# Sharing six PSUM banks between two attention passes: four and two in place of three and three

## The reference

```python
# part a, for each of 3 scales; 16 heads of width 8
q, k, v = proj(Wq, bq), proj(Wk, bk), proj(Wv, bv)
scores = einsum('bhqd,bhkd->bhqk', q, k) * sqrt(8)
scores = where(causal, -inf, scores)
m = max(scores, axis=-1)
e = exp(scores - m)
out = (e / (sum(e) + 1e-6)) @ v           # then @ Wo.T + bo, layer norm
# the 3 scales are joined by Wout and a second layer norm
# part b: one such attention, scores / sqrt(8) plus slope[h] * (key - query)
# layers: 6 x (windowed attention, window 32, heads of width 64; then a gated feed-forward)
```

## Time and profile before

| | |
|---|---|
| time, median of 3 | 5068.25 us |
| the profiled execution's own time | 5069.97 us |
| its span, first to last instruction | 5068.2 us |
| PE busy | 4611.6 us, 91% |
| DVE busy | 3758.7 us, 74% |
| ACT busy | 3280.8 us, 65% |
| POOL busy | 2201.0 us, 43% |
| mean granted clock of PE | 0.941 |

### The profile page before, as it was taken

How to read it: one execution, slowest core, us unless ns; L and a number is a source line. 1 busy time by engine, 2 the same in 40 slices (tenths; PEclk the granted TensorE clock), 3 DMA queues, 4 the chain that set the end, 5 groups by cost and what they waited for, 6 DMA issues and landing times. The chain is left out here.

```text
span 5068.2 us, 123490 instructions
## 1 busy us (share of the span) xinstructions
PE 4611.6 (91%) x50168; PEld 2728.4 (54%) x50168; DVE 3758.7 (74%) x5802; ACT 3280.8 (65%) x5283; POOL 2201.0 (43%) x1271
## 2 busy tenths in 40 slices
PE   5999989869999999999999499789999999999997
PEld 2333334336666666666666234256666666666664
DVE  4877777258888888888887287278888887888884
ACT  1666666437777777777776146367777777777774
POOL 1111000046656565565654010166556565656551
PEclk5999999779999999999999679699999999999998
DMA  3221120000000000000000220000000000000000
GB/s 79 42 41 34 31 36 3 2 32 10 10 15 10 5 21 2 19 7 15 10 6 2 48 41 2 32 10 10 2 15 10 15 10 15 10 2 24 2 6 9
DMA packets 70041, 87.85 MB, mean 17 GB/s; under 512 B 22533, under 2 KB 44289, under 8 KB 68865
## 3 DMA queue, kind: packets, MB, share of 16 engines
q1 hardware_dynamic: 67720, 76.41, 6.5%
q10 hardware_dynamic: 1728, 3.15, 0.3%
HBM read 65.11 MB, written 13.63 MB: 16 GB/s over the span
## 5 line engine op out<-in xcount | busy, mean ns | idle before, releaser
L1077 PE MATMUL ps<-l_wqk,l_xa 128*128 128x512 f32 x1536 | 768.3, 623 | 51.7 <-DVE l_rs L1523 40.2
L674 DVE TENSOR_REDUCE a_pm<-ps 128x1 f32<-128x512 f32 (+3 forms) x912 | 561.7, 657 | 204.2 <-PE ps L568 199.1
L1184 PE MATMUL ps<-l_yb,l_mh 128*128 128x256 f32 x3072 | 709.8, 381 | 0.0
L772 ACT ACTIVATE a_pt<-ps 128x512 f32<-128x512 f32 x864 | 475.2, 600 | 328.0 <-PE ps L574 325.9
L1480 POOL TENSOR_TENSOR l_pn<-l_pe,l_rl 128x1024 f32<-128x1024 f32 x192 | 365.2, 1902 | 616.0 <-DVE l_rl L1561 616.0
L1184 PEld LDWEIGHTS ps<-l_yb,l_mh 128*128 128x128 f32 x3072 | 564.3, 190 | 71.5 <-issue 2.4
L1324 ACT ACTIVATE l_sq<-ps 128x1024 f32<-128x1024 f32 x384 | 389.9, 1015 | 317.4 <-PE ps L1077 317.4
L1523 DVE TENSOR_TENSOR l_rs<-ps,l_tab 128x512 f32<-128x512 f32 x768 | 491.0, 681 | 0.0
L1077 PEld LDWEIGHTS ps<-l_wqk,l_xa 128*128 128x128 f32 x1536 | 277.0, 194 | 384.5 <-issue 337.1
L1471 POOL TENSOR_TENSOR l_qkn<-l_rc,l_rn 128x1024 f32<-128x1024 f32 x192 | 386.4, 2013 | 203.3 <-DVE l_rn L1541 203.3
L1463 POOL TENSOR_TENSOR l_rc<-l_rc,l_rs 128x1024 f32<-128x1024 f32 x192 | 451.5, 2352 | 41.5 <-DVE l_rs L1523 41.5
(11 more groups left out here) (222 smaller groups left out, 8771.5 us busy)
## 6 DMA issues: line engine op xcount, KB each, us to landing
l_wqk<-in_lWqkv SPq DMA_DIRECT2D x24, 512.0 KB, 3.6
scratch<-a_parts SPq DMA_DIRECT2D x12, 768.0 KB, 4.2
a_qs<-scratch SPq DMA_DIRECT2D x72, 128.0 KB
a_ks<-scratch SPq DMA_DIRECT2D x60, 128.0 KB
l_wvt<-in_lWvT SPq DMA_DIRECT2D x12, 512.0 KB, 5.0
l_wo<-in_lWo SPq DMA_DIRECT2D x12, 512.0 KB, 7.2
l_w<-in_lW SPq DMA_DIRECT2D x12, 341.0 KB, 2.9
scratch<-b_parts SPq DMA_DIRECT2D x4, 768.0 KB, 4.9
```

The costliest lines, as they stand in the source:

```text
L674: nc.vector.tensor_reduce(to, src, AX.X, ALU.max).then_inc(s1_free, 1)
L772: nc.scalar.activation(pt[:, K % 3, n - GROUPS[k][0], :], ps[:, 3 + N2 % 3, :], ACT.Exp).then_inc(s2_free, 1)
L1077: last = nc.tensor.matmul(ps[:, x, :], xa[:, u, o:o + P], wqk[:, a * INNER + x * CH:a * INNER + (x + 1) * CH], start=True, stop=True)
L1184: last = nc.tensor.matmul(ps[:, 6, 0:2 * P], mh[:, h, :], yb[:, n % 2, h, :], start=h == 0, stop=h == LH - 1, skip_group_check=True)
```

## The change

The first pass gets banks 0 to 3 and the second pass banks 4 and 5. PE issues an item of the first pass when the item four before it has been read, and one of the second pass when the item two before it has been read. Matmuls, reductions, exponentials, their order and all other waits stay as they are.

```diff
-                                bank1 = N1 % 3
+                                bank1 = N1 % 4
...
-                                if N1 >= 3:
-                                    pe.wait_ge(s1_free, N1 - 2)
+                                if N1 >= 4:
+                                    pe.wait_ge(s1_free, N1 - 3)
...
-                                bank2 = 3 + N2 % 3
+                                bank2 = 4 + N2 % 2
...
-                                if N2 >= 3:
-                                    pe.wait_ge(s2_free, N2 - 2)
+                                if N2 >= 2:
+                                    pe.wait_ge(s2_free, N2 - 1)
...
-                            src = ps[:, N1 % 3, 0:len(item) * w].rearrange("p (j n) -> p j n", n=w)
+                            src = ps[:, N1 % 4, 0:len(item) * w].rearrange("p (j n) -> p j n", n=w)
...
-                            nc.scalar.activation(pt[:, K % 3, n - GROUPS[k][0], :], ps[:, 3 + N2 % 3, :], ACT.Exp).then_inc(s2_free, 1)
+                            nc.scalar.activation(pt[:, K % 3, n - GROUPS[k][0], :], ps[:, 4 + N2 % 2, :], ACT.Exp).then_inc(s2_free, 1)
```

## The result

The changed kernel takes 5156.49 us, the median of four runs (5148.00 to 5165.98), against 5071.82 for the kernel before in four runs: 1.0164 times as long, with a 95% interval of 1.0151 to 1.0177. The forecast was 5136 with a range of 5095 to 5200. Direction, mechanism and range were right; the loss was 85 us where 68 were forecast. Between the two profiled executions it is 89 us (5159.29 against 5069.97), and 86 of them lie in the 28 mixed steps, where the sum had 58. The four steps with a second pass alone are 3 us longer, the first-pass-only steps 3 us shorter, and the layers together 6 us longer (0.2%).

A forecast was written before the change was run, and what follows sets the result against it. No engine is full; in-order PE, 91% busy, sets the pace when it waits. Mixed steps lose 43 us in "a" and 15 in "b", second-pass-only steps 10: 68 us, so 5138, or 5136 against the median; range 5095 to 5200.

The forecast's parts named there:

- second pass alone: Four steps without a first pass: two banks cost 0.5 us a group, five groups, 2.5 us a step, 10 us.
- C at 1.13 us after A: Second-pass matmul of a group's third item waits for the first item's exponential: 0.48 + 0.60 + 0.05, formerly 0.44 us.
- D at 1.62: Second-pass matmul of a group's fourth item starts 0.49 us after the third's, 1.62 us after the first's, formerly 1.22.
- The group 0.40 longer: Group of four items, 22-25, in a mixed step: grows by 1.62 - 1.22 = 0.40 us, passed on in full.
- plain: Mixed steps without side work, like q = 1: seven groups lose 2.8 us a step; 8 in "a", 4 in "b".
- q = 0: Mixed steps where projections cover items 10 to 19: loss 1.4 us each, four counted in "a".
- q = 2: Mixed steps where a 0.66 us side piece hides the wait in most groups: loss 1.4 us each, five in "a".
- q = 3: Mixed steps with, in "a", a layer norm that stops everything anyhow: 1.6 us each, five; "b", without norm, 2.4.
- The cover by side pieces: Side work between a group's items hides the new wait, so q = 0 and q = 2 steps lose 1.4 us, not 2.8.
- the first rival: PE's clock falls too: 66 us more in plain mixed steps, about 5205; 5170 for half, 5290 in all 28; chance 0.16.
- ACT has enough slack: Rival: ACT, idle 272 of 769 us in mixed steps of "a", can give a bank away; 5068, no change; chance 0.06.
- DVE's waits decide: Rival: second pass does not hold PE, and its waits for DVE's maxima go; 5070 - 35 = 5035; chance 0.04.

The follow-up runs named there:

- e1: Against the kernel before: second pass cut from three banks to two, first pass kept at three, bank 3 idle; 5156.53 us (1.0148).
- e3: The kernel before, three and three banks, with each second-pass exponential taking only the first 256 of its 512 columns; 5007.66 us (0.9870).
- e4: The changed kernel, four and two banks, with each second-pass exponential taking only the first 256 of its 512 columns; 5064.64 us (0.9978).

## Why the prediction was right, and where it was off

**The second pass with two banks: right, by its own steps.** C at 1.13 us after A: measured 1.23. D at 1.62: measured 1.72. The group 0.40 longer: measured 0.49. The term that was mis-sized is PE's reaction behind a freed bank, read as 0.05 us from a single row; here it is 0.14. e1 shows that this bank is the whole loss, and e3 and e4 that C and D follow ACT's exponential.

**Steps, against the sum.** From the ends of the steps in both traces:

| kind of step | number | forecast | measured |
|---|---|---|---|
| "a", plain | 8 | 22.4 | 27.7 |
| "a", q = 0 | 4 | 5.6 | 8.3 |
| "a", q = 2 | 5 | 7.0 | 8.0 |
| "a", q = 3 | 5 | 8.0 | 18.2 |
| "b", plain | 4 | 11.2 | 18.9 |
| "b", q = 2 and 3 | 2 | 3.8 | 4.3 |
| second pass alone | 4 | 10 | 3.1 |
| first pass alone | 2 | 0 | about -3 |

A plain step whose clock stays at 1.00 lost 2.6 to 3.0 us, with 2.8 forecast, six of them in all: the 0.09 us too little in each group and the groups that hide more than I counted cancel. The cover by side pieces was real, 1.6 us with q = 2 and, with q = 0, 1.9 in two of four (0.9 and 3.6 in the others), against 1.4 and 1.4. With a second pass alone the group was right and its step was not. A long group went from 3.75 to 4.24 us (in the kernel after, below, 1017.22 to 1021.46), the 0.5 of the forecast, but in four groups of a step and not in five; that would be 8 us. And the clock fell later there, with 81 us at the lower level in place of 91, which by an estimate at 0.35 us each hid some 4 of them. So this row came out at 3 and not at 10, a miss that the total hides. One step counted as plain (q = 1, 41.3 us before) holds a second layer norm and lost 1.9.

```profile
1017.22 1.09 ACT L772 ACTIVATE a_pt<-ps 128x512 f32<-128x512 f32 x2 [1.86 <-PE ps L574]
...
1021.46 1.09 ACT L772 ACTIVATE a_pt<-ps 128x512 f32<-128x512 f32 x2 [1.86 <-PE ps L574]
```

**The clock: the step that failed.** The sum had nothing for it, and the first rival too much. The excess sits in the plain steps with a fall of the clock (+5.1 and +6.9 in "a", three of +5.4 in "b") and in the norm steps. The same step of "b" in the kernel after and in e1_3_2, where the clock stayed up:

```profile
3065.00:3099.30 34.30, 29.75 (x306) 11.83 (x305) 23.86 (x41) 21.07 (x38) 1.74 (x5) 0.90 0.01 2
...
3080.00:3085.00 5.00, 4.59 (x47) 1.77 (x40) 2.53 (x4) 2.31 (x5) 0.00 (x0) 0.52 0.01 3
```

```profile
3072.70:3104.70 32.00, 27.16 (x306) 11.15 (x305) 23.82 (x41) 21.10 (x38) 1.74 (x5) 1.00 0.01 2
```

A clock of 0.90 over 34.3 us is 6.9 us at the lower level (1.2 GHz, a granted 0.50), and the step is 2.3 us longer: 0.34 us lost for each of them, since PE's waits fill a part of the slow time. By the same reckoning, step by step, the 28 mixed steps have 53 us at the lower level before and 115 after; 62 more, at 0.34, are 21 of the 28 us by which the sum fell short in them. In the norm steps of "a" it is 31 before and 58 after, which makes 9 us, nearly the whole excess of that row. This is a reckoning over the steps and not an experiment. Its price does not rest on one pair: three more steps that differ between the kernel after and e1_3_2 in the clock alone give 0.33 to 0.37, and two give 0.5. The clock fell more than I gave it, in a minority of the steps and not in the whole stage: my mark for the rival, a granted clock under 0.95, was reached by 0.01. Why it falls in one plain step and stays up in its like is open.

The page "TensorE: Matmul & The Clock Gate" of the Trainium skill, section "A second HAM failure mode: psum-queue depth-cycling", has the rule that PE's short idle stretches between groups can make the clock swing; the trace agrees in that it now swings in more steps than before, and not in that it does so in each step of the pattern: those at 536.4 and 570.0 us hold 1.00.

**The first pass with four banks.** In the norm step L550's wait went and nothing came of it, as forecast. In the first-pass-only steps I counted nothing; they went from 28.2 to 26.5 us (with three banks, in e1, they stay at 28.2), so DVE was in part what they waited for, at a clock of 0.50 too. There are two such whole steps, 3 us in all. The wait of L550 went with three banks as well (e1), so it was the second pass that took it over, and not the fourth bank that removed it.

**The signs.** I wrote that L574 and L563 would be seen waiting for ACT and that the waits of the earlier trace rows would nearly go. Only L550's did. The label was no evidence on either side.

**The rivals.** That ACT has enough slack falls: ACT was idle for a third of the mixed steps, and two banks still cost 85 us. That DVE's waits decide falls for this split: C and D are held by ACT, and taking the fourth bank away again cost nothing. What a fourth bank would gain while the second pass keeps three stays open, since no run has four and three.

## What to carry to other kernels

A bank is held for the distance from one burst's matmul to the end of its reader's work on it, so two of three banks can be too few for an engine that is busy 65% of the time; before moving one, take from the timeline when the reader ends, not how busy it is. A wait behind two engines that end together is booked on one of them: change one side's depth or length before believing the list. And where PE waits for a copy, look at the copy's place in its engine's queue first; here moving two copies by one or two places was worth 1.2 or 1.45%, and none of the three other splits of the banks was worth anything. Then split such a gain by stage and look at the clock of each: about half of this one was clock that came back in 4 steps of 32.

## What the runs showed of the hardware that was not expected

- Value matmuls (128 rows, 32 columns a head, 512 wide, f32) of four heads overlap on PE: two heads took 0.98 us, four took 1.00. Half the width of all four took 0.57.
- PE's matmul starts 0.05 to 0.14 us after the end of the exponential that frees its bank.
- Exponentials of 512 columns take about 0.60 us each but start 0.49 us apart when they queue; of 256 columns they take 0.38.
- The clock's lower level cost about 0.34 us for each microsecond at it in the mixed steps (a step of 34.3 us against 32.0), and 0.35 in the long groups of the second pass alone (3.75 us against 2.45), where PE at the low clock was busy 35.0 of 36.8 us.
